# An attention, mixer and feed-forward block: the planner's steps written out call by call, other banks, other engines

## The reference

```
q, k, v = x Wq' + bq, x Wk' + bk, x Wv' + bv      # 16 query heads, 4 key heads, 16 wide
q, k = rope(rms_norm(q)) * gain, rope(rms_norm(k))
x1 = layernorm(x + softmax(causal(q k' / 4)) v Wo' + bo)
x2 = layernorm(x1 + wkv(time_decay, time_first, k=x1, v=ctx))  # a scan over the tokens
y  = layernorm(x2 + relu(x2 sign(up)' * up_scale) sign(down)' * down_scale * output_scale)
```

## Time and profile before

| | |
|---|---|
| three runs | 251.81 us median, 248.95 to 255.6 |
| profiled execution | 254.29 us, its span 252.5 us |
| granted TensorE clock, mean | 0.894 |
| PE busy | 193.0 us, 76% |
| DVE busy | 171.2 us, 68% |
| POOL busy | 160.6 us, 64% |
| ACT busy | 135.5 us, 54% |

### The profile page before, as it was taken

How to read it: one execution, slowest core, us unless ns; L and a number is a source line. 1 busy time by engine, 2 the same in 40 slices (tenths; PEclk the granted TensorE clock), 3 DMA queues, 4 the chain that set the end, 5 groups by cost and what they waited for, 6 DMA issues and landing times. The chain is left out here.

```text
span 252.5 us, 3753 instructions
## 1 busy us (share of the span) xinstructions
PE 193.0 (76%) x1176; PEld 113.9 (45%) x1176; DVE 171.2 (68%) x325; ACT 135.5 (54%) x246; POOL 160.6 (64%) x195
## 2 busy tenths in 40 slices
PE   2556698998767999699989784999949761969460
PEld 1221133535235466456655551566537650757340
DVE  2966315679958957976998699378838829944640
ACT  2232537885753699267936671479537462365500
POOL 7641304192693698388649984773892997495755
PEclk9857579999997999799999997799997998699975
DMA  4795040421501801220140114010010000010111
GB/s 113 216 423 120 3 85 22 105 51 44 148 0 45 148 0 42 44 65 3 43 101 12 42 42 96 14 58 31 3 42 3 0 17 25 0 44 0 42 42 43
DMA packets 19213, 14.98 MB, mean 59 GB/s; under 512 B 14314, under 2 KB 14570, under 8 KB 18925
## 3 DMA queue, kind: packets, MB, share of 16 engines
q1 hardware_dynamic: 19180, 14.53, 21.0%
HBM read 9.29 MB, written 2.10 MB: 45 GB/s over the span
## 5 line engine op out<-in xcount | busy, mean ns | idle before, releaser
L833 POOL TENSOR_TENSOR hid_lo<-hid,hid_hi 128x512 f16<-128x512 f32 x24 | 33.6, 1401 | 19.8 <-ACT hid_hi L714 19.8
L521 PE MATMUL banks<-dn_sb,hid_hi 128*128 128x256 bf16 x128 | 34.5, 302 | 13.2 <-DVE hid_lo L1125 13.0
L653 ACT ACTIVATE probs<-banks 128x1024 f32<-128x1024 f32 x32 | 32.7, 1022 | 16.4 <-PE banks L352 16.4
L305 PE MATMUL banks<-wqkv_sb,xT_sb 128*128 128x384 f32 x64 | 29.7, 621 | 9.1 <-DMA wqkv_sb<-wqkv_dram 4.7
L521 PE MATMUL banks<-dn_sb,hid_lo 128*128 128x256 bf16 x128 | 34.3, 302 | 0.0
L707 ACT ACTIVATE hid<-banks,ups_man 128x256 f32<-128x256 f32 x64 | 26.8, 474 | 12.8 <-PE banks L500 12.4
L500 PE MATMUL banks<-x2hi,up_sb 128*128 128x256 f16 x128 | 31.8, 286 | 0.0
L500 PE MATMUL banks<-x2lo,up_sb 128*128 128x256 f16 x128 | 31.7, 286 | 0.0
L348 PE MATMUL banks<-rows 32*128 32x512 f16 x128 | 20.6, 401 | 10.8 <-ACT probs L653 4.7
L827 POOL TENSOR_TENSOR newt<-ratio,rec 128x512 f32<-128x512 f32 x8 | 10.2, 1270 | 26.9 <-ACT rec L692 26.9
L305 PEld LDWEIGHTS banks<-wqkv_sb,xT_sb 128*128 128x128 f32 x64 | 15.8, 253 | 20.1 <-issue 16.2
(11 more groups left out here) (107 smaller groups left out, 394.3 us busy)
## 6 DMA issues: line engine op xcount, KB each, us to landing
xT_sb<-xT_dram SPq DMA_DIRECT2D x8, 256.0 KB, 3.1
x_sb<-x_dram SPq DMA_DIRECT2D x8, 256.0 KB, 4.6
ctxT_sb<-ctxT_dram SPq DMA_DIRECT2D x8, 256.0 KB, 2.6
out_dram<-outb SPq DMA_DIRECT2D x8, 256.0 KB, 2.0
up_f<-up_dram SPq DMA_DIRECT2D x1, 1024.0 KB, 7.5
dn_f<-down_dram SPq DMA_DIRECT2D x1, 1024.0 KB, 9.5
wqkv_sb<-wqkv_dram SPq DMA_DIRECT2D x1, 384.0 KB, 3.4
wo_sb<-wo_dram SPq DMA_DIRECT2D x1, 256.0 KB, 3.9
```

The source lines that it names most:

```text
L305: nc.tensor.matmul(banks[:, PJ + t, 0:E], xT_sb[:, p % 2, c, t, :], wqkv_sb[:, c, :], start=(c == 0), stop=False)
L521: mm = nc.tensor.matmul(banks[:, DN, t * D:(t + 1) * D], part[:, j, t * S:(t + 1) * S], dn_sb[:, j, :], start=(j == 0 and t == 0 and m == ...
L653: nc.scalar.activation(probs[:, 2 * m:2 * m + 2].rearrange("p n j s -> p n (j s)"), banks[:, SC:SC + 2], ACT.Exp).then_inc(sems["probs_don ...
L833: nc.gpsimd.tensor_tensor(hid_lo[:, 2 * n:2 * n + 2], hid[:, 2 * n:2 * n + 2], hid_hi[:, 2 * n:2 * n + 2], ALU.subtract).then_inc(sems["hi ...
```

## The change

- The step functions are gone. Each engine's calls stand in one flat list, in an order that differs from pair to pair; PE's list is cut in eight sections, each under one `pe.If`. The waits for a bank stand in this list.
- The banks: `PJ, AC, WO, X1, ZT, X2, DN = 2, 5, 0, 4, 2, 5, 0`, `UP = (5, 5, 3, 3)`, and `SC = (6, 0, 6, 6)`: the second of the four score calls uses banks 0 and 1.
- The mask: a score call now has four products of 64 rows by 256 columns (one per half of the queries' positions and bank), on rows 0 to 63 for the first bank and 64 to 127 for the second.
- From POOL to DVE: `normed` of the first and third norm, `rope_sum`, `newton_rms` (four operations now), `low_bits` of n = 0 and 3. From DVE to POOL: `scale_heads` and `add_out`. Each n of `low_bits` has its own semaphore.
- The bias split is four DVE operations on 97 rows (parts in rows 0, 64, 96); `pick` is gone, and two fills by DVE stand before.
- ACT issues the bias loads, those of the norm constants and the identity at its start, and all later loads of xT, x and context; SP keeps the first loads, the transposing transfers and the stores.

The core of the diff:

```diff
-        LO_POOL, LO_DVE = (0, 2, 3), (1,)
-        PJ, AC, WO, X1, ZT, X2, DN = 2, 2, 4, 0, 4, 1, 5
+        PJ, AC, WO, X1, ZT, X2, DN = 2, 5, 0, 4, 2, 5, 0
         PV = (1, 5)
-        UP = (4, 3, 1, 2)
-        SC = 6
+        UP = (5, 5, 3, 3)
+        SC = (6, 0, 6, 6)
...
+                mm = [None, None]
+                for h in range(2):
+                    for s in range(2):
+                        r = HALF * s
+                        mm[s] = nc.tensor.matmul(banks[:, SC[m] + s].rearrange("p (j s) -> p j s", j=REP)
+                                                 [:, :, h * HALF:(h + 1) * HALF],
+                                                 later[r:r + HALF, h, :], masked[r:r + HALF],
+                                                 start=False, stop=(h == 1 and not guarded))
                 for s in range(2):
-                    mm = nc.tensor.matmul(banks[:, SC + s], id_b[:], mask_sb[:].rearrange("p j s -> p (j s)"),
-                                          start=False, stop=not guarded)
...
+            project(0)
+            pe.wait_ge(sems["qk_out"], 1)
+            pe.wait_ge(sems["v_out"], 1)
+            project(1)
+            pe.wait_ge(sems["qk_out"], 2)
+            pe.wait_ge(sems["v_out"], 2)
+            project(2)
...
+                scores(0, 0, guarded)
+                scores(0, 1, guarded)
...
+                pe.wait_ge(sems["o3_done"], 1)
+                pe.wait_ge(sems["att_done"], 9)
+                scores(5, 1, guarded)
...
+            act.wait_ge(bias_ones, 1)
+            for r in (0, 64, 96):
+                act.dma_start(bias_in[r:r + 1], biases.unsqueeze(0)).then_inc(bias_in_done, 16)
+            for dst, src in norm_consts:
+                act.dma_start(dst, src).then_inc(norm_in, 16)
+            act.dma_start(id_f[:], ident_in).then_inc(ident_done, 16)
             nc.scalar.preload_act_table_set("natural_log_exp_and_others")
...
+            take_heads(0)
+            squares(0)
+            take_values(0)
+            next_xT(2)
+            first_guess(0)
+            take_heads(1)
+            high_heads(0)
+            take_values(1)
...
+            def scale_heads(p):
+
+                done(pool, "rscale_done", p)
+                done(pool, "rot_done", p)
+                freed(pool, "lo_done", p)
+                nc.gpsimd.tensor_tensor(qn[:], rot[:], rscale[:].unsqueeze(2).to_broadcast([128, T * NQK, HD]),
+                                        ALU.mult).then_inc(sems["qn_done"], 1)
...
+            normed(0, 7, r1, x1, "x1_done")
+            moments(1, 6, z)
+            normed(1, 6, z, x2[:, 0], "x2_done")
+            scan(7)
+            mix(7)
+            low_bits(5, 1)
+            moments(2, 4, r3)
```

More of the change, by code:

```diff
@@ L767, in _ @@
-            for i in range(23):
-                step(i)
+            take_heads(0)
[6 more added lines that the diff above has]
+            take_values(1)
+            next_xT(3)
+            squares(1)
+            take_heads(2)
+            first_guess(1)
+            mixer_constants()
+            exps(0, 0)
+            exps(0, 1)
+            exps(0, 2)
+            squares(2)
@@ L1206, in _ @@
[L1206 to L1209 removed]
+            split_biases()
+            gains_constants()
+            head_sums(0)
+            rope_sines(0)
+            rope_cosines(0)
+            newton_rms(0)
+            rope_sum(0)
+            small_constants()
+            low_heads(0)
+            swap_keys(0)
+            guard_flag.append(dve.value_load(guard[0:1, 0:1], min_val=0, max_val=1))
@@ new lines, in _ @@
+            attend_norm(1, 1)
+            scan(0)
+            mix(0)
+            rope_cosines(4)
+            rope_sines(4)
+            num_by_rec(0)
+            residual(1)
+            moments(0, 1, r1)
+            refine(0)
+            head_sums(4)
+            add_mixed(0)
+            normed(0, 1, r1, x1, "x1_done")
+            with dve.If(guard_flag[0]):
+                row_maxima(3)
+            rope_sum(4)
+            newton_rms(4)
+            attend_norm(2, 0)
+            moments(1, 0, z)
@@ new lines, in _ @@
+            attend_norm(2, 1)
+            normed(1, 0, z, x2[:, 0], "x2_done")
+            scan(1)
+            low_heads(4)
+            mix(1)
+            rope_cosines(5)
+            swap_keys(4)
+            low_x2(0)
+            with dve.If(guard_flag[0]):
+                row_maxima(4)
+            rope_sines(5)
+            num_by_rec(1)
+            residual(2)
+            moments(0, 2, r1)
+            refine(1)
+            head_sums(5)
+            add_mixed(1)
+            normed(0, 2, r1, x1, "x1_done")
@@ new lines, in _ @@
+            rope_sum(5)
+            newton_rms(5)
+            attend_norm(3, 0)
+            moments(1, 1, z)
+            attend_norm(3, 1)
+            normed(1, 1, z, x2[:, 1], "x2_done")
+            low_heads(5)
+            scan(2)
+            low_bits(0, 0)
+            mix(2)
+            low_bits(0, 1)
+            rope_cosines(6)
+            residual(3)
+            low_x2(1)
+            moments(0, 3, r1)
+            num_by_rec(2)
+            head_sums(6)
+            refine(2)
@@ new lines, in _ @@
+            scan(3)
+            low_bits(1, 1)
+            mix(3)
+            low_heads(6)
+            rope_cosines(7)
+            rope_sines(7)
+            residual(4)
+            low_x2(2)
+            head_sums(7)
+            num_by_rec(3)
+            swap_keys(6)
+            moments(0, 4, r1)
+            low_bits(1, 3)
+            with dve.If(guard_flag[0]):
+                row_maxima(6)
+            rope_sum(7)
+            refine(3)
+            add_mixed(3)
+            normed(0, 4, r1, x1, "x1_done")
```

1318 lines of the change are left out of this document (903 added, 415 removed).

## The result

The changed kernel takes 249.55 us in the median of 20 runs (242.09 to 255.94), against 252.45 (248.95 to 255.93) for the kernel before in its 20. The ratio is 0.9705, with a 95% interval from 0.9634 to 0.9777: faster by 3%. It compares the fast runs alone, and of the changed kernel's 20 only three count as such (242.09, 244.3 and 245.7 us); by the medians of all runs the change gives 1.1%. The profiled execution is the quickest of the 20, 242.09 us with a span of 240.2, and the rows of the kernel after are all from it. The forecast of 239 lies 1% under that one and 4% under the median; the range, 227 to 252, holds both. By the comparison a 251.81 us kernel becomes 244.4.

What follows compares the result with a forecast made beforehand. The prediction took the kernel to be bound by its fixed order, with long ends. Fill 48, middle 151 and tail 40 gave 239 us of span, 240.8 profiled, 238.4 on the runs' footing, stated as 239; range 227 to 252.

Steps and rivals of the forecast that it cites:

- the middle: Between first and last x1 writing: 151 us for 150.9, added DVE work taking what the removed waits give.
- Two bank pairs: Scores: the second tile need not wait for the first's exponent; booked at nothing either way.
- scores standing for o3: Bank 0 is shared, so a pair's second scores wait for o3 and the residual; booked at nothing.
- DVE's work: DVE's busy time over the whole kernel rises from 171.2 to 191.8 us, making it the busiest engine.
- The fill: Start up to the first x1: 48 us instead of 53.1, by earlier bias, values' copy and pair 2's projection.
- The loads on ACT: Load issues moved to ACT, at the start and later: bounds 0 and 11 us, taken at 1.
- The tail: Stretch behind the last x1: 40 us instead of 48.5, with DVE's wait for POOL's output gone.
- Rival A: DVE's two-input operations and POOL's exclude each other; 34 us less, span 218; chance 0.13.
- Rival B: DVE's waits move and don't vanish, the middle keeps 34 us idle; 250.4 us, no change; chance 0.22.
- Rival C: Low parts queue behind DVE's other work and hold PE in ffn_down; 26 us more, 265; chance 0.13.

Runs made afterwards that it cites:

- e1: The changed kernel with one pe.If around all eight sections of PE's list instead of one around each: 222.75 us, ratio 0.8855.
- e7: e1 with the second bank pair undone, all four score tiles on banks 6 and 7: 251.47 us, ratio 1.0003.
- e8: e1 with the first and third norm's subtraction and scaling back on POOL: 236.98 us, ratio 0.9453.
- e9: e1 with sixteen low parts (n = 0 and 3) back on POOL: 239.21 us, ratio 0.9435.
- e11: e1 with the later loads of xT, x and context issued by SP instead of ACT: 218.65 us, ratio 0.8619.
- e10: e1 with the rope sum back on POOL, ahead of scale_heads: 223.8 us, ratio 0.8769.
- e5: The changed kernel with one copy of the list and forty short branches around only what the guard adds: 224.3 us, ratio 0.8873.
- e3: The changed kernel with sixteen pe.If instead of eight, each section cut again behind its scores: 243.41 us, ratio 0.9597.
- e12: The changed kernel with its eight long branches moved behind projections of pairs 3 to 7 and two ffn_down products: 231.37 us.

## Why the prediction was right, and where it was so by luck

**Direction and size held, by two errors that cancel.** The sum had no term for the branches. Taking seven of them out gives 20 us by the spans (240.2 to 220.3) and 27 by the medians. And its middle was too long: without these branches (e1) the middle is 129.2 us and not 151, with 6.0 us of DVE idle for 22 forecast and 123.2 of work for 129. The second bank pair, booked at nothing, is a large part of that, since taking it out costs 29 us (e7). So about 20 us too little stood beside 22 too many. With one bank pair e7 stands at the kernel before, 1.0003, so in this list all the rest of the change brings nothing without the second pair. Undoing parts one at a time doesn't add up, since the list was laid out for the whole: e7, e8 and e9 alone are 59 us worse than e1 together, and the kernel before is 31.

**The step that failed is the cover.** I read that the sections of the list begin at the scores, and never asked what PE has queued there. The busy shares can't show it: "issue" did not bound the kernel before because the loop ended its guarded body behind a projection.

**Two bank pairs, "nothing either way".** The reasons given, PE, ACT and DVE all below full and one such tile for a pair, judge a wait by shares. e7 shows fourteen waits of 1.4 us, and products at half their speed behind the one shown. Of what I feared in exchange, scores standing for o3, e1 shows nothing: 2.6 us for exponents is the largest wait of L314.

**DVE's work.** By their rows the moved operations add 13.6 (norms, 466 ns and not 373), 9.4 (low parts, 783 and not 900), 6.3 (Newton, 0.2 as taken) and 6.5 us, less 15.2: 20.6, for 22.0 forecast. The engine's busy time rose by only 14.7, to 185.9 and not 191.8. The rows of neighbouring instructions overlap at their ends, and busy time counts an overlap once: all groups of DVE sum to 201 us after and 181 before, for 185.9 and 171.2 busy, and the two sums differ by 20 us, as the terms do. Terms from means are therefore a little too large. POOL came to 89.1 for 92.

**The fill**, 51.0 for 48. Pair 2's projection did move. The first copy came at 10.46 for 11.18, 0.7 us and not 1.5, because the bias operations start later (5.59 for 4.94) and the first of the four takes 2.04 us on 97 rows; I had given it the mean of operations on 3 rows. The loads on ACT hold 1.8 us more (e1 to e11: 50.1 to 48.3), which brings it to the forecast.

**The tail**, 40.7 for 40, with DVE busy for 26.9 of the 28.8 counted. It stays so in e1 and e11. Here DVE's wait for POOL's output is gone as forecast, and the tail is 7.8 us shorter. But that the output norm moved to DVE is not what shortened it: e8 has that norm on POOL again, with r3 on POOL too, and its tail behind the last x1 (191.4 to 233.3) is 41.9 us, e1's 41.0. No run put r3 back on DVE.

**The middle**, 148.5 for 151, is right for a wrong reason: its DVE idle time, 24.4 us for 22 forecast, was the branch and not leftover chains.

**Rival A** (218): the contention is real (e9, e10: busy time does not fall when work leaves), and e1, with DVE at 95% of the middle, and e11 at 218.65 come near its number. But the sum of exclusive times was not shown to be the bound, and the kernel as changed did not run at it. Its term of 3.2 us a pair for DVE also doesn't follow from the terms above it, which give 22.0 by 8, or 2.75, and with that 214 for 218. The Trainium skill, "SBUF — State Buffer", "Who interferes with whom", has two-input VectorE operations and GpSimd's reads exclude each other. e9's longer scan agrees with it. The x1 norms of e10 have one tensor input and two columns of scalars, and they slow beside POOL's sum too (466 to 718 ns in the mean); the same section counts such operations among those that can take the shared ports, in their two-port modes, and no run here shows in which mode they ran. **Rival B** (250) was right that waits would come back under other names, and wrong on their cause. **Rival C** (265) fell: PE waits 4.5 us for the low parts, not 39, and moving them back is what costs (e9).

**Open:** what sets the border between a short and a long jump; why the clock fell behind four of the six gaps and not behind the other two; what a list laid out for one bank pair would reach; why the runs of the kernel after spread over 242 to 256 us at granted clocks of 0.866 to 0.92 while e1's spread over 3.4.

## What to carry to other kernels

When a list is cut into guarded copies, ask at each cut what the engine has queued: branch once, guard only the added parts, or put the cut behind queued products that last as long as the branch. Look for "issue" among PE's waits before pricing anything else, and look behind each gap of PE for a lower granted clock, which is a second cost. A wait that comes several times for each pair is priced by its times and its length, not by whether the engines' shares leave room.

## What the runs showed of the hardware

- A compare-and-branch on PE's queue took 0.2 us in the median over 37 skipped instructions (e5). In e3 it took 0.3 to 0.4 us over a skipped copy of 121 to some 300 instructions and 2.8 to 3.8 us over most longer ones, and in each long one, and in no short one, a 16 KB instruction packet was fetched. The longest was 5.3 us (e12). DVE's took 56 to 67 ns.
- Behind some gaps of 1.7 to 3 us PE's products ran slower, down to half their speed: a projection 5.35 us for 2.75, an up product 0.42 for 0.27. Behind others of 1.6 and 2.65 us they did not. The mean granted clock of the middle was 0.93 with the gaps and 0.99 without.
- DVE's busy time did not change when 6.5 us (e10) or sixteen operations of some 0.78 us (e9) went to POOL; the operations left took longer.
- 64-row mask products of 256 columns do run in pairs, yet gained 0.12 us a tile for the 0.27 of half their columns.
